# Attention A in three runs of head pairs, with the projected output kept in PSUM over a run and the norm of three groups inside the slots

## The reference, cut to what matters

```python
# x: (8, 256, 256) float32; H = 16 heads, q/k width 128 (64 plain + 64 rotary), v width 128
def attn_a(x, q_a_w, q_b_w, kv_a_w, kv_b_w, o_w):
    q = x @ q_a_w.T @ q_b_w.T                  # 16 heads of 64 + 64
    ckv = x @ kv_a_w.T                         # 64 shared + 64 rotary
    kvb = ckv[..., :64] @ kv_b_w.T             # per head: 64 of k, 128 of v
    query, key = concat(q_pass, rope(q_rot)), concat(k_pass, rope(k_rot))
    attn = softmax(einsum('bhqd,bhkd->bhqk', query, key), axis=-1)
    out = einsum('bhqk,bhkd->bhqd', attn, v)
    return out.reshape(B, S, H * 128) @ o_w.T  # a sum over the heads
x = x + attn_a(layernorm(x), ...)
x = x + ffn(layernorm(x), ...)
x = x + attn_b(layernorm(x), ...)
x = x + ffn(layernorm(x), ...)
```

## Time and profile before

| | |
|---|---|
| median of 3 runs | 1533.96 us (1531.46 to 1535.32) |
| the profiled execution, its own time | 1535.29 us |
| its span, first to last instruction | 1533.5 us |
| mean granted clock | 0.987 |
| busy: PE, DVE, ACT, POOL | 95%, 76%, 55%, 40% of the span |
| HBM read and written | 37.56 MB, 2.23 MB |
| slot 0's `normalise` | at 79.82 us |
| attention A's last instruction, the experts' first | about 396.5 us, 396.83 us |

### The profile page before, as it was taken

The page is one execution under the profiler, slowest core; times in us unless marked ns, Lnnn a source line. Parts: engine busy times, 40 slices in busy tenths (PEclk is TensorE's granted clock), DMA queues, the critical chain, the costliest instruction groups (busy, mean ns, idle before and its releaser), DMA issues. The chain is left out here.

```text
span 1533.5 us, 26670 instructions
## 1 busy us (share of the span) xinstructions
PE 1463.5 (95%) x8904; PEld 1262.6 (82%) x8904; DVE 1171.0 (76%) x2661; ACT 835.8 (55%) x2040; POOL 612.6 (40%) x484
## 2 busy tenths in 40 slices
PE   8899999998799999988999999999999879999998
PEld 6677777776688888877899999989999868888887
DVE  7889999999765555587888888888888777555554
ACT  4788888885432333326766666666666433333322
POOL 2577777875100000017766666666666210000000
PEclk9899999999999999998999999999999999999999
DMA  2265555555210000003222222213222200010001
GB/s 101 53 161 142 154 145 151 148 129 149 82 41 22 22 21 0 1 1 91 62 70 61 71 63 64 75 42 80 73 50 49 56 22 21 21 42 21 0 0 56
DMA packets 73155, 100.16 MB, mean 65 GB/s; under 512 B 10304, under 2 KB 63552, under 8 KB 73024
## 3 DMA queue, kind: packets, MB, share of 16 engines
q1 hardware_dynamic: 73024, 98.55, 24.3%
HBM read 37.56 MB, written 2.23 MB: 26 GB/s over the span
## 5 line engine op out<-in xcount | busy, mean ns | idle before, releaser
L1834 DVE TENSOR_TENSOR f_hidden<-ps,f_silu 128x512 f32<-128x512 f32 x128 | 87.6, 689 | 201.7 <-PE ps L122 201.6
L481 POOL TENSOR_TENSOR ab_swapped<-ab_swapped,const 128x512 f32<-128x512 f32 x126 | 162.9, 1293 | 167.6 <-ACT ab_swapped L476 167.6
L1725 ACT ACTIVATE f_silu<-ps 128x512 f32<-128x512 f32 x128 | 76.3, 598 | 276.8 <-PE ps L122 276.8
L120 PE MATMUL ps<-xh,f_wl 128*128 128x512 f32 x512 | 203.2, 397 | 1.6 <-DVE f_hidden L1834 1.6
L121 PE MATMUL ps<-xl,f_wh 128*128 128x512 f32 x512 | 202.8, 396 | 0.0
L122 PE MATMUL ps<-xh,f_wh 128*128 128x512 f32 x512 | 202.5, 396 | 0.0
L1536 POOL TENSOR_TENSOR ab_qk<-ab_qk,ab_swapped 128x512 f32<-128x512 f32 x126 | 172.5, 1369 | 9.9
L1304 ACT ACTIVATE ab_probs<-ab_probs,ab_negmax 128x128 f32<-128x128 f32 (+1 forms) x256 | 114.6, 448 | 82.6 <-DVE ab_negmax L1407 80.6
L73 POOL TENSOR_TENSOR rstd<-shifted,minus_half 128x4 f32<-128x4 f32 x16 | 16.2, 1013 | 339.6 <-DVE shifted L67 339.6
L771 ACT ACTIVATE aa_probs<-ps,aa_negmax 128x256 f32<-128x256 f32 x256 | 119.2, 471 | 47.1 <-DVE aa_negmax L846 44.0
L120 PE MATMUL ps<-f_wh,f_hl 128*128 128x256 f32 x512 | 144.2, 282 | 0.4 <-DVE x L1850 0.4
(11 more groups left out here) (210 smaller groups left out, 4377.5 us busy)
## 6 DMA issues: line engine op xcount, KB each, us to landing
ab_probsT<-ab_squares SPq DMA_DIRECT2D x128, 192.0 KB, 3.6
aa_probsT<-f_stages SPq DMA_DIRECT2D x128, 128.0 KB, 2.6
b_stages<-keys SPq DMA_DIRECT2D x128, 128.0 KB, 2.7
f_stages<-wf_in SPq DMA_DIRECT2D x16, 768.0 KB, 4.5
aa_spread<-aa_inv_line SPq DMA_DIRECT2D x64, 128.0 KB, 3.0
b_stages<-wb_qkv_in SPq DMA_DIRECT2D x8, 768.0 KB, 6.3
a_stage<-wa_in SPq DMA_DIRECT2D x8, 608.0 KB, 4.3
x<-x_in SPq DMA_DIRECT2D x4, 512.0 KB, 7.0
```

The lines of the kernel that those rows point to most:

```text
L120: nc.tensor.matmul(out, ll, rh, start=start, stop=False)
L481: return engine.tensor_tensor(by_batch(out), by_batch(src), table(c, rows, col), ALU.mult)
L1834: nc.vector.tensor_tensor(hidden[:, m, :], UP(m), silu[:, m, :], ALU.mult).then_inc(hid_done, 1)
```

## The change

The slots get a new order. `RUN_HEADS` makes three runs: head pair 0, pairs 1 to 3, pairs 4 to 7. Within a run each token group goes through all head pairs of the run before the next group comes. `output` opens an accumulation in `OUT(0)` and `OUT(1)` with the first slot of a group's run and closes it with the last, and only then `add_out` adds the two banks to `x`: 24 adds in place of 64. All weights of a head pair are folded at one place, and the folded ones of more pairs are kept: the added buffers lie in corners of `c.xh` and `c.xl` that are not yet in use. `FOLD_SLOT` and `LOAD_SLOT` are new tables of slots. The norms of groups 0 to 2 are made inside slots 21 to 31; group 3's statistics come at the end.

```diff
+    RUN_HEADS = [(0,), (1, 2, 3), (4, 5, 6, 7)]
-        at = lambda n: (n // NG, n % NG)
+        RUNS = [(it, s) for its in RUN_HEADS for s in range(NG) for it in its]
+        RUN_OF = [run * NG + s for run in range(len(RUN_HEADS)) for s in range(NG) for _ in RUN_HEADS[run]]
+        at = lambda n: RUNS[n]
+        opens = lambda n: n == 0 or RUN_OF[n] != RUN_OF[n - 1]
+        closes = lambda n: n == SLOTS - 1 or RUN_OF[n] != RUN_OF[n + 1]
-        def fold_after(n):
-            it, s = at(n)
-            return it + 2 if s == NG - 1 and it + 2 < HP else None
+        FOLD_SLOT = {2: 0, 3: 1, 4: 5, 5: 10, 6: 12, 7: 14}
+        LOAD_SLOT = {2: 0, 3: 1, 4: 2, 5: 6, 6: 11, 7: 13}
+        folds = {n: it for it, n in FOLD_SLOT.items()}
+        loads = {n: it for it, n in LOAD_SLOT.items()}
+        FINISH = {4 * g + 2 * HP + 5: g for g in range(NG - 1)}
+        finish = lambda n: FINISH.get(n)
...
         @block.sync
-                if s == 2 and it + 2 < HP:
-                    load(it + 2)
+                if n in loads:
+                    load(loads[n])
...
         @block.tensor
+            def fold(it):
                 pe.wait_ge(stage_in, 16 * (it + 1))
-                if it > 1:
-                    pe.wait_ge(wo_lo, it)
+                pe.wait_ge(wo_lo, it)
                 fold_product(nc, FOLD(it)[:, 0:P], stage, 0).then_inc(fold_ready, 1)
+                pe.wait_ge(fold_ready, it)
+                fold_product(nc, FOLD(it)[:, P:2 * P], stage, 1)
+                fold_output_product(nc, FOLD(it)[:, 2 * P:], stage).then_inc(wo_ready, 1)
...
+                if opens(n):
+                    after(pe, out_added, 2 * RUN_OF[n] + i - 1)
-                    ins = matmul3(nc, bank[:, t * D:(t + 1) * D], (mh[:, s % 2, tok], ml[:, s % 2, tok]), (woh[:, half, :], wol[:, half, :]), True, True)
+                    ins = matmul3(nc, OUT(i)[:, t * D:(t + 1) * D], (mh[:, n % 2, tok], ml[:, n % 2, tok]), (woh[it], wol[it]), opens(n) and t == 0, closes(n) and t == 1)
...
+            def turn_rows(g, k):
+                if k == 0:
+                    pe.wait_ge(norm.normed_done, g + 1)
+                after(pe, norm.lo_done, KD * g + k)
+                if g == 0:
+                    pe.wait_ge(wo_lo, HP)
+                for i in range(TG):
+                    ins = nc.tensor.transpose(FOLDED[:, i * P:(i + 1) * P], norm.normed[:, i, k * P:(k + 1) * P], c.ident)
+                ins.then_inc(norm.turned, 1)
...
-                if j == 1 and fold_after(n):
-                    fold_query(fold_after(n), n)
-                if j == 1 and s == 1 and it + 1 < HP:
-                    pe.wait_ge(fold_lo, it + 1)
-                    fold_output(it + 1, FOLDED)
+                if j == 3 and n in folds:
+                    fold(folds[n])
+                if j == 2 and finish(n - 1) is not None:
+                    turn_rows(finish(n - 1), 0)
+                if j == 0 and finish(n - 2) is not None:
+                    turn_rows(finish(n - 2), 1)
...
         @block.scalar
+                if j == 0 and n - 1 in folds:
+                    fold(folds[n - 1])
+                if j == 3 and finish(n - 1) is not None:
+                    norm_upper(finish(n - 1), 0)
+                if j == 1 and finish(n - 2) is not None:
+                    norm_upper(finish(n - 2), 1)
...
         @block.vector
+                if j == 0 and n - 1 in folds:
+                    fold(folds[n - 1])
-                if j in (1, 2) and n >= 2:
+                if j in (1, 2) and n >= 2 and closes(n - 2):
                     add_out(n - 2, j - 1)
+                if j == 2 and finish(n) is not None:
+                    normalise_stats(finish(n))
+                if j == 0 and finish(n - 1) is not None:
+                    norm_rows(nc, c, norm, dve, finish(n - 1))
+                if j == 3 and finish(n - 1) is not None:
+                    norm_lower(finish(n - 1), 0)
+                if j == 1 and finish(n - 2) is not None:
+                    norm_lower(finish(n - 2), 1)
...
         @block.gpsimd
                     mixed_lo(n - 1)
+                if n - 1 in folds:
+                    fold_rest_parts(folds[n - 1])
...
+                if finish(n) is not None:
+                    norm_rstd(nc, c, norm, pool, finish(n))
+                    pool.wait_ge(norm.rstd_done, finish(n) + 1)
```

More of the change, by code:

```diff
@@ L501, in project_a @@
     g = slice(s * G, (s + 1) * G)
[L502 to L506, removed]
+    upper, lower = a.wh[half], a.wl[half]
+    nc.tensor.matmul(out, lower[:, 0, h, :], a.q1h[:, g], start=True, stop=False)
+    nc.tensor.matmul(out, upper[:, 0, h, :], a.q1l[:, g], start=False, stop=False)
+    nc.tensor.matmul(out, lower[:, 1, h, :], a.q2[:, g], start=False, stop=False)
+    nc.tensor.matmul(out, upper[:, 1, h, :], a.q2[:, g], start=False, stop=False)
+    return nc.tensor.matmul(out, upper[:, 0, h, :], a.q1h[:, g], start=False, stop=True)
 def fold_output_product(nc, bank, stage):
@@ L710, in step @@
                     mix(n, 1)
-                if n == SLOTS - 1 and j == 0:
-                    pe.wait_ge(rope_read, 2 * SLOTS)
-                    pe.wait_ge(swap_done, 2 * SLOTS)
-                    norm_turn(nc, c, norm, pe, 0, norm_banks)
+                if j == 2 and finish(n - 1) is not None:
+                    turn_rows(finish(n - 1), 0)
+                if j == 0 and finish(n - 2) is not None:
+                    turn_rows(finish(n - 2), 1)
             for j in range(2):
-                scores(0, 0, j)
+                scores(0, j)
             for h in range(2):
@@ L721, in _ @@
             for j in range(2, PAIRS):
-                scores(0, 0, j)
-            fold_query(1, 0)
+                scores(0, j)
+            fold(1)
             for j in range(LEAD - PAIRS):
-                scores(0, 1, j)
+                scores(1, j)
             for n in range(SLOTS):
@@ L792, in step @@
                     queries_hi(n + 3, j - 2)
-                if n == SLOTS - 1 and j == 0:
-                    norm_hi(nc, c, norm, act, 0, norm_banks)
             swap(1, 0)
             swap(1, 1)
-            exps(0, 0, 0)
+            exps(0, 0)
             queries_hi(1, 0)
-            exps(0, 0, 1)
+            exps(0, 1)
             swap(2, 0)
             queries_hi(1, 1)
-            exps(0, 0, 2)
+            exps(0, 2)
             swap(2, 1)
-            exps(0, 0, 3)
-            fold_query(1)
-            exps(0, 1, 0)
+            exps(0, 3)
+            fold(1)
+            exps(1, 0)
             queries_hi(2, 0)
-            exps(0, 1, 1)
+            exps(1, 1)
             queries_hi(2, 1)
@@ L901, in step @@
                     invert(n + 1)
-                if last and s >= 2 and j == 2:
-                    normalise_stats(s - 2)
-                if last and s >= 2 and j == 3:
-                    norm_rows(nc, c, norm, dve, s - 2)
-                if last and s == 3 and j == 1:
-                    norm_lo(nc, c, norm, dve, 0, norm_banks)
+                if j == 2 and finish(n) is not None:
[6 more added lines that the diff above has]
+                    norm_lower(finish(n - 2), 1)
             nc.vector.memset(inv[:], 0.0)
@@ L935, in _ @@
                     step(n, j)
[L936 removed]
             normalise(SLOTS - 1)
[L938 to L943 removed]
+            add_out(SLOTS - 1, 0)
+            add_out(SLOTS - 1, 1)
             normalise_stats(NG - 1)
[L945 removed]
         @block.gpsimd
@@ L1000, in _ @@
                         queries_lo(n + 3, h)
-                if n + 2 >= SLOTS:
-                    norm_rstd(nc, c, norm, pool, n + 2 - SLOTS)
-                    pool.wait_ge(norm.rstd_done, n + 3 - SLOTS)
-                if fold_after(n):
-                    fold_rest_parts(fold_after(n))
+                if finish(n) is not None:
+                    norm_rstd(nc, c, norm, pool, finish(n))
+                    pool.wait_ge(norm.rstd_done, finish(n) + 1)
             mixed_lo(SLOTS - 1)
-            for s in range(2, NG):
-                norm_rstd(nc, c, norm, pool, s)
+            norm_rstd(nc, c, norm, pool, NG - 1)
 PARTS_B = [slice(0, 2), slice(2, 3)]
```

168 lines of the change are left out of this document (70 added, 98 removed).

## The result

| | before | after |
|---|---|---|
| median of the runs (6 each) | 1535.04 us | 1545.45 us |
| ratio | | 1.0069 [1.0054, 1.0084] |
| span of the profiled execution | 1533.5 us | 1544.3 us |
| mean granted clock | 0.987 | 0.983 |

The account below looks back on a forecast made before the run. DVE was taken to bound the slots, with PE, ACT, POOL and SP close behind. Slots 4 to 28 -3.3, first slots +5.8 and end -3.0 gave -0.5: 1533.5 us, no change, range 1521 to 1542.

Parts of the forecast that it names:

- adds gone, less the other queues: Slots 4 to 28: 34 fewer adds at 0.59 us save 20.1, of which other engines' limits take back 5.6.
- old folds gone: Slots 4 to 28: folds at their former places vanish, 2.7 us a head pair, -14.4.
- new folds: Slots 6, 11, 13, 15: four folds at their new places, 2.0 us each, +8.0.
- SP's hold: Slots 4 to 28: the load waits for POOL's fold and delays SP's spread, 1.0 to 1.7 us a slot, +6.2 in all.
- norm of groups 0 and 1: Slots 21 to 27: statistics, products and subtractions on DVE, 4.5 us a group, +9.0.
- port: Slots 4 to 28: norm products beside POOL, one meeting a group, +2.4; as rival all four meet, +10, chance 0.07.
- The other queues: Slots 4 to 28: without adds PE's 8.7 us limits plain slots, losing 0.43 in each of 13 intervals, +5.6.
- The rival in which it grows: Rival: the load delays the spread by its own 4.2 us, each of four holds costs 4.5, 1543 us; chance 0.07.
- the first slots: Start of attention A: PE waits for weights, earlier folds and the spread lengthen slots, +5.8, ends +2 and +8.
- the end: Slot 29 to the experts' block: less norm work left at the end, -3.0, ends -6 and +1.
- DVE's saving arrives: Rival: plain slots run at 8.3 us and SP's hold and PE's weight waits hide, 1518.7 us; chance 0.17.

Follow-up runs that it names:

- e4: Kernel after, with every slot's output added at once again (64 adds instead of 24): 1554.60 us, ratio 1.0116 to the kernel before.
- e3: Kernel after, with later weight loads and POOL held back during the norm's products: 1533.04 us, ratio 0.9982 to the kernel before.
- e1: Kernel after, with the weight loads of head pairs 4 to 7 one slot later: 1538.56 us, ratio 1.0017 to the kernel before.
- e5: e3 without the product of the mix's lower half with the upper output weights (PE) in slots inside a run: plain slots 8.96 to 9.00 us.
- e6: e3 with DVE's product of swapped rows and sines cut to a sliver from slot 16's projection on: plain slots 8.48 to 8.64 us.
- e2: Kernel after, with POOL waiting for the norm's products before its lower half of the mix: 1539.67 us, ratio 1.0030 to the kernel before.
- e10: e3 with 20 instead of 12 idle products before the last output: 8.75 us from last `normalise` to the experts' first cast, 9.12 in e3.

## Why the prediction was wrong, point by point

Slots 4 to 28 by the terms of the sum, each from the experiment or the rows that move it:

| term | forecast | measured | from |
|---|---|---|---|
| adds gone, less the other queues | -20.1 + 5.6 = -14.5 | -7.1 | e4 |
| old folds gone | -14.4 | -14.7 (not run alone) | rows of before: 250.99 less 25 x 9.45 |
| new folds | +8.0 | +8.4 | e3: slots 5, 10, 12, 14 less 9.45 or 8.98 |
| SP's hold | +6.2 | +6.9 | after against e1: slots 6, 7, 11 to 14 |
| norm of groups 0 and 1 | +9.0 | +9.5 | e3: slots 21, 22, 25, 26 less 9.45 or 8.99 |
| port | +2.4 | +4.3 | e3 against e1: slots 22, 26 |
| slot 23 | 0 | +1.2 | after against e1 |
| sum | -3.3 | +8.5 (+7.8 as a whole) | |

The terms come from different kernels, and 0.7 us of their sum is not placed.

**The step that failed is "The other queues", with the adds' price ahead of it.** I priced an add at 0.59 from its row, then let PE's 8.7 cut part of that off. e4 gives 0.23 an add, and 7.4 of the 11.1 us missing in this stretch are here. The bound I named was the wrong one: e5 took 0.9 us off PE in a stretch of three slots and moved nothing, and e6 ran below 8.7 with PE's work whole. VectorE bounded the slot before and after, but not by the sum of its busy time: its product of sines ends where POOL's operation ends plus 0.55, and by the rows of slots 17 and 18 an add ahead of that point is free. The 9.28 busy of 9.45 that I read as a full engine had half a microsecond of standing still inside that product. These are the rows of the kernel before, in the same slot 28: 1.12 us, of which 0.56 lie behind POOL's end (357.47), where the product takes 0.69 in slots in which it meets no POOL operation.

```profile
356.19 1.28 POOL L963 TENSOR_TENSOR a_raw<-a_raw,a_swapped 64x512 f32<-64x512 f32 x1
356.91 1.12 DVE L481 TENSOR_TENSOR a_swapped<-a_swapped,const 64x512 f32<-64x512 f32 x1
```

I had cited the rule that explains it, for the norm's products, and not asked which instruction of the plain slot it applies to.

**The port** was mis-sized: I took one meeting a group, three of four products met, and the row I took it from had POOL idle for 1.83 before its one operation. Measured 4.3 for 2.4, and slot 23 below. As a rival it had its mechanism right and 0.07 of chance; its price of 4 x 1.0 more a group was too high, since the products themselves lengthen by 3.1 and 2.1 of it reach the interval. By the rule in the Trainium skill, "SBUF — State Buffer", "Who interferes with whom", such a product and any POOL operation exclude each other for a whole instruction; the trace agrees (4.46 against 1.38), and also with its line that an operation with two inputs in SBUF meets POOL's reads.

**The hold** came near the forecast sum (+6.9 for +6.2) by luck, by two errors that nearly cancel: each cost 2.5 to 3.0 and not 1.0 to 1.7 (the squares behind the load took 3.49 for the 2.7 of my chain, and from the spreads' issue at 143.62 to `normalise` passed 4.17 for my 3.65), and 0.4 to 0.5 came back each time in the slot behind. The rival in which it grows was half right, for its size only.

**Slot 23** took 10.21 in the kernel after and 9.01 in e1, with the same instructions. In e2, without the collision, it took 8.98. In slot 22 of the kernel after TensorE idled 2.81 us during the collision, did four transposes, idled 1.09 more, and then stepped at 0.21, its 1.2 GHz level, with 0.77 as the mean clock of the slot. The two stretches are slots 22 and 23; the column behind POOL's is the clock:

```profile
297.68:311.45 13.77, 9.87 (x53) 8.15 (x52) 12.83 (x20) 8.41 (x26) 8.94 (x8) 0.77 0.42 96
311.45:321.66 10.21, 10.21 (x74) 8.67 (x73) 8.55 (x17) 8.62 (x26) 7.34 (x7) 0.98 0.49 128
```

The kernel after's slot 26 had 0.88 and was followed by 8.99, e1's slots 22 and 26 had 0.88 and 0.75 and were followed by 9.01 and 9.48. In these four the lag behind a collision goes with the clock. But e2's slots 22 and 26 had 0.85 without a collision and were followed by 8.98 and 8.98, so a low clock alone did not make the lag; no run changed the clock alone, and the cause stays open.

**Right:** 24 rows of adds; slots with folds; the first slots (+4.7 for +5.8) with PE waiting 2.13 for the weights; `normalise` waiting for the spread; the end (-1.8 for -3.0, with PE at its lower clock in the last output, which is dearer by 1.1 than the same stretch in e10). "DVE's saving arrives" was the furthest off, and it had the second highest chance.

## What to carry to other kernels

Before an instruction's time is counted as a gain, look for a point behind it whose end another engine fixes; work ahead of such a point can be free, work behind it is not, and two neighbouring slots with and without the work show which is which (6.00 against 5.99 here). A VectorE operation with both inputs in SBUF beside a busy GpSimd was such a point here. A DMA issue that waits for a late event belongs behind whatever its queue still owes to the current step: one slot later it cost 0.4 to 0.5 us a time and gave back 7 us net.

## What the runs showed of the hardware that was not expected

- A product of 64x32 elements lasted 0.73 us beside a GpSimd operation and 0.19 where it began just ahead of that operation's end (e6). A small instruction stood still as long as a large one would have; only what it did behind the other's end was less, 0.05 us for 0.55. The profile counts the standing still as busy time.
- It was not always VectorE that waited. In slot 13 of the kernel after its product began 0.20 ahead of GpSimd's two rotations and took 0.69, and they took 3.00 together, where one takes 1.29 as a rule (median) and up to 1.74:

```profile
213.07 0.69 DVE L481 TENSOR_TENSOR a_swapped<-a_swapped,const 64x512 f32<-64x512 f32 x1 [0.48 <-ACT a_swapped L470]
213.27 3.00 POOL L956 TENSOR_TENSOR a_raw<-a_raw,a_swapped 64x512 f32<-64x512 f32 x2
```

- Row maxima that read PSUM (0.65 to 0.69) and the transposes (0.69 to 0.71) kept their time beside GpSimd's operations throughout; of VectorE's frequent instructions only the sines' product and the norm's products lengthened.
- In slot 22 of the kernel after, where the four products took 4.46 us, TensorE idled 2.81 us for them and 1.09 behind its transposes, and its next matmuls stepped at 0.21 instead of 0.12.
